# Sorted experts on four places per buffer, and the copy of a tile's gate and up weights split between ScalarE and VectorE

## The reference

```
h = jax.nn.silu(flat @ W1[e]) * (flat @ W3[e])
out = out + cw[:, e:e + 1] * (h @ W2[e])
```

```
act_BSEF = jax.nn.silu(gating_BSEF)
fuse_BSEF = act_BSEF * up_BSEF
out_BSD = jnp.einsum('BSED,BSE->BSD', down_BSED, full_weights_BSE)
```

## Time and profile before

| | us |
|---|---|
| median of 3 runs | 2033.66 (2028.91 to 2034.36) |
| span of the profiled execution | 2032.1 |
| first sorted phase, first load to landing of the last scatter | 1581.2 to 1723.2 |
| second sorted phase, the same | 1860.0 to 2001.3 |

### The profile page before, as it was taken

How to read it: one execution, slowest core, us unless ns; L and a number is a source line. 1 busy time by engine, 2 the same in 40 slices (tenths; PEclk the granted TensorE clock), 3 DMA queues, 4 the chain that set the end, 5 groups by cost and what they waited for, 6 DMA issues and landing times. The chain is left out here.

```text
span 2032.1 us, 46788 instructions
## 1 busy us (share of the span) xinstructions
PE 1596.6 (79%) x16783; PEld 1170.4 (58%) x16783; DVE 1134.2 (56%) x3048; ACT 850.6 (42%) x1634; POOL 564.9 (28%) x782
## 2 busy tenths in 40 slices
PE   5788999999488879699987777888886787343892
PEld 3645666666266647488875454555553686332882
DVE  5755677776554447355544586867773343642333
ACT  2322456555211125244423265655552675002663
POOL 4111011111111103433202211232333354464553
PEclk9989899999699989799988897988895899556996
DMA  4000222221099100000001002222220242211224
GB/s 171 1 2 16 63 59 54 59 58 33 20 323 325 39 1 1 2 4 3 3 2 64 1 1 74 68 68 63 70 56 21 70 113 74 94 49 45 73 75 145
DMA packets 84683, 124.99 MB, mean 62 GB/s; under 512 B 17328, under 2 KB 70576, under 8 KB 82928
## 3 DMA queue, kind: packets, MB, share of 16 engines
q1 hardware_dynamic: 75824, 104.30, 17.6%
q0 software_dynamic: 8640, 17.78, 2.7%
HBM read 67.47 MB, written 55.59 MB: 61 GB/s over the span
## 5 line engine op out<-in xcount | busy, mean ns | idle before, releaser
L1527 DVE TENSOR_REDUCE small<-ps 128x8 f32<-128x1024 f32 (+1 forms) x256 | 312.7, 1224 | 120.6 <-PE ps L1313 70.7
L1454 ACT ACTIVATE scr<-ps 128x1024 f32<-128x1024 f32 x256 | 262.3, 1024 | 237.3 <-PE ps L1288 121.4
L244 POOL TENSOR_TENSOR rstd<-vare,neghalf 128x4 f32<-128x4 f32 (+1 forms) x72 | 63.3, 879 | 542.4 <-DVE vare L223 541.1
L2812 POOL DMA_INDIRECT results<-scr x142 | 136.3, 960 | 154.7 <-DVE scr L2801 67.2
L1326 PE MATMUL ps<-scr 128*32 128x256 f32 x2048 | 173.9, 414 | 0.2 <-ACT scr L1454 0.2
L1275 PEld LDWEIGHTS ps<-scr_r 32*128 32x128 f32 x1024 | 82.3, 195 | 154.9 <-ACT scr L1454 87.6
L1275 PE MATMUL ps<-scr_r 32*128 32x256 f32 x1024 | 136.4, 345 | 35.0 <-ACT scr L1454 21.5
L2733 PE MATMUL ps<-scr 128*128 128x128 f32 x1136 | 155.6, 281 | 2.4 <-ACT scr L2760 1.4
L1306 PE MATMUL ps<-scr_r 32*128 32x256 f32 x1024 | 137.9, 351 | 10.5 <-DMA scr_r<-scr_r 5.9
L2733 PEld LDWEIGHTS ps<-scr 128*128 128x128 f32 x1136 | 142.8, 197 | 3.9 <-issue 3.8
L2794 DVE TENSOR_TENSOR scr<-ps,scr 128x256 f32<-128x256 f32 x142 | 60.3, 425 | 138.2 <-ACT scr L2779 107.6
(11 more groups left out here) (410 smaller groups left out, 3537.0 us busy)
## 6 DMA issues: line engine op xcount, KB each, us to landing
scr_r<-scr_r SPq DMA_DIRECT2D x512, 64.0 KB
rows_m<-kinds SPq DMA_DIRECT2D x8, 2064.0 KB, 30.7
rows_f<-kinds SPq DMA_DIRECT2D x8, 2064.0 KB, 74.9
scr<-results SPq DMA_DIRECT2D x32, 256.0 KB
scr<-rows_m SPq DMA_DIRECT2D x71, 64.5 KB
scr<-rows_f SPq DMA_DIRECT2D x71, 64.5 KB
scr<-in_l3m SPq DMA_DIRECT2D x1, 3072.0 KB, 10.0
results<-scr POOLq DMA_INDIRECT x142
```

What stands on the lines that cost most here:

```text
L244: pool.tensor_tensor(k.rstd[:, 0:self.J], k.vare[:, 0:self.J], k.neghalf[:, 0:self.J], ALU.pow).then_inc(self.e["rstd_ready"].sem, 1)
L1454: act.activation(PT[:, g % 2, 2 * x:2 * x + 2, :], ps[:, 4:6, :], ACT.Exp).then_inc(e["prob_ready"].sem, 1)
L1527: dve.tensor_reduce(nf[:, half, 0:blocks, at:at + 2].rearrange("p q a -> p a q"), ps[:, 2 * (p % 2):2 * (p % 2) + 2, :].rearrange("p a (q ...
L2812: pool.indirect_dma_start(results, bass.IndirectOffsetOnAxis(ap=names[:, j % IN, P:P + 1], axis=0), y[:, j % OUT, :], None).then_inc(store ...
```

## The change

It does these things, all in `phase_sorted_experts`:

- `xT`, `sil`, `hT` and `here` get four places (`DEEP = 4`), `xin` 16 instead of 8. `here` and `y` move to another SBUF region. `turned` and the gate and up products get three PSUM banks each, the projections keep two.
- TensorE's order becomes gate and up of tile j, transposition of j + 4, projection of j - 3.
- ScalarE copies only the gate half of the weights (128 x 256), for tile j + 3, after SiLU j, and copies the transposed rows of j + 3 before SiLU j.
- VectorE copies the up half (128 x 256), with its own register load, for tile j + 3, after the product of tile j and before the eviction of tile j - 3. The up products wait for it by a new semaphore, `up_kept`.

The core of the diff:

```diff
-    e = k.signals(SORTED, turned=1, xt_ready=1, kept=1, gu_ready=1, act_ready=1, h_ready=1, out_ready=1, out_read=1)
-
-    IN, OUT = 8, 4
+    e = k.signals(SORTED, turned=1, xt_ready=1, kept=1, up_kept=1, gu_ready=1, act_ready=1, h_ready=1, out_ready=1, out_read=1)
+
+    IN, OUT, DEEP = 16, 4, 4
...
-    xin, xT, sil, hT, y, here = k.carve((IN, P + 1), (2, P), (2, 2 * P), (2, 2 * P), (OUT, P), (2, 2, 2 * P))
+    xin, xT, sil, hT = k.carve((IN, P + 1), (DEEP, P), (DEEP, 2 * P), (DEEP, 2 * P))
+    here, y = k.carve((DEEP, 2, 2 * P), (OUT, P), base=k.scr2[:, 6144:8704])
...
+    def turned_at(j):
+        return ps[:, j % 3, 0:P]
+    def hidden_at(j):
+        return ps[:, 3 + j % 3, :]
+    def out_at(j):
+        return ps[:, 6 + j % 2, 0:P]
...
         def turn(j):
             arrived(pe, j)
-            wait(pe, "xt_ready", j - 2)
-            pe.transpose(ps[:, j % 2, 0:P], xin[:, j % IN, 0:P], cst["ident"]).then_inc(e["turned"].sem, 1)
+            wait(pe, "xt_ready", j - 3)
+            pe.transpose(turned_at(j), xin[:, j % IN, 0:P], cst["ident"]).then_inc(e["turned"].sem, 1)
 
         def gate_up(j):
             wait(pe, "xt_ready", j)
             wait(pe, "kept", j)
-            wait(pe, "h_ready", j - 2)
+            wait(pe, "h_ready", j - 3)
             for n in range(2):
+                if n:
+                    wait(pe, "up_kept", j)
...
-        for j in range(-2, SORTED + 1):
+        for j in range(-4, SORTED + 3):
             if there(j):
                 gate_up(j)
-            if there(j + 2):
-                turn(j + 2)
-            if there(j - 1):
-                project(j - 1)
+            if there(j + 4):
+                turn(j + 4)
+            if there(j - 3):
+                project(j - 3)
...
-            wait(act, "gu_ready", j - 2)
-            act.activation(here[:, j % 2], gate_up_of[:, :, bass.ds(at, 256)], ACT.Copy).then_inc(e["kept"].sem, 1)
+            wait(act, "gu_ready", j - DEEP)
+            act.activation(here[:, j % DEEP, 0, :], gate_up_of[:, 0, bass.ds(at, 256)], ACT.Copy).then_inc(e["kept"].sem, 1)
...
-        for j in range(-2, SORTED):
+        for j in range(-3, SORTED):
...
+            if there(j + 3):
+                keep_turned(j + 3)
             if there(j):
                 wait(act, "gu_ready", j)
-                wait(act, "h_ready", j - 2)
-                act.activation(sil[:, j % 2, :], ps[:, 2 + j % 2, 0:256], ACT.Silu).then_inc(e["act_ready"].sem, 1)
-            if there(j + 2):
-                keep_turned(j + 2)
-                keep_weights(j + 2)
+                wait(act, "h_ready", j - DEEP)
+                act.activation(sil[:, j % DEEP, :], hidden_at(j)[:, 0:256], ACT.Silu).then_inc(e["act_ready"].sem, 1)
+            if there(j + 3):
+                keep_weights(j + 3)
 
     def dve(dve):
+        dve.wait_ge(arrive, 16 * pieces)
+
+        def keep_up(j):
+            at = dve.value_load(d.table[0:1, 0, j:j + 1], min_val=0, max_val=7 * 256)
+            wait(dve, "gu_ready", j - DEEP)
+            dve.tensor_copy(here[:, j % DEEP, 1, :], gate_up_of[:, 1, bass.ds(at, 256)]).then_inc(e["up_kept"].sem, 1)
+
+        for j in range(DEEP - 1):
+            keep_up(j)
         d.shift(dve)
-        for j in range(SORTED + 1):
+        for j in range(SORTED + 3):
...
+            if there(j + 3):
+                keep_up(j + 3)
```

More of the change, by code:

```diff
@@ L2707, in arrived @@
             eng.wait_ge(loads[j % 4].sem, loads[j % 4].at(j // 4))
+    def turned_at(j):
[4 more added lines that the diff above has]
+        return ps[:, 6 + j % 2, 0:P]
     def sp(sp):
         for j in range(SORTED):
[L2711 to L2712 removed]
+            if load and j >= 16 and j % 4 == 0 and j < 16 + 4 * PIECES:
+                load(sp, (j - 16) // 4)
             row = sp.value_load(d.table[0:1, 1, j:j + 1], min_val=0, max_val=8 * ROWS + 6 * P)
@@ L2729, in gate_up @@
             wait(pe, "kept", j)
-            wait(pe, "h_ready", j - 2)
+            wait(pe, "h_ready", j - 3)
             for n in range(2):
+                if n:
+                    wait(pe, "up_kept", j)
                 for c in range(2):
-                    ins = pe.matmul(ps[:, 2 + j % 2, 256 * n + P * c:256 * n + P * c + P],
-                                    here[:, j % 2, n, P * c:P * c + P], xT[:, j % 2, :], start=True, stop=True)
+                    ins = pe.matmul(hidden_at(j)[:, 256 * n + P * c:256 * n + P * c + P],
+                                    here[:, j % DEEP, n, P * c:P * c + P], xT[:, j % DEEP, :], start=True, stop=True)
             ins.then_inc(e["gu_ready"].sem, 1)
@@ L2792, in dve @@
                 wait(dve, "act_ready", j)
-                wait(dve, "out_ready", j - 2)
-                dve.tensor_tensor(hT[:, j % 2, :], ps[:, 2 + j % 2, 256:512], sil[:, j % 2, :],
+                wait(dve, "out_ready", j - DEEP)
+                dve.tensor_tensor(hT[:, j % DEEP, :], hidden_at(j)[:, 256:512], sil[:, j % DEEP, :],
                                   ALU.mult).then_inc(e["h_ready"].sem, 1)
-            if there(j - 1):
-                wait(dve, "out_ready", j - 1)
-                landed(dve, j - 1 - OUT)
-                out = ps[:, 4 + (j - 1) % 2, 0:P]
+            if there(j + 3):
+                keep_up(j + 3)
+            if there(j - 3):
+                wait(dve, "out_ready", j - 3)
+                landed(dve, j - 3 - OUT)
+                out = out_at(j - 3)
                 if scale is None:
-                    ins = dve.tensor_copy(y[:, (j - 1) % OUT, :], out)
+                    ins = dve.tensor_copy(y[:, (j - 3) % OUT, :], out)
                 else:
-                    ins = dve.tensor_tensor(y[:, (j - 1) % OUT, :], out, scale, ALU.mult)
+                    ins = dve.tensor_tensor(y[:, (j - 3) % OUT, :], out, scale, ALU.mult)
                 ins.then_inc(e["out_read"].sem, 1)
```

10 lines of the change are left out of this document (4 added, 6 removed).

## The result

The changed kernel took **2046.08 us** (median of 6 runs, 2037.64 to 2055.41) beside 2034.01 us for the kernel before (6 runs): a ratio of 1.0078, 95% interval 1.0046 to 1.0109. Slower by 12 us where 27 us less were forecast, and outside the range. The profiled execution has a span of 2044.6 us beside 2032.1.

The account below looks back on a forecast made before the run. SyncE's load queue was taken as the next bound at 1.67 us a tile: 33.0 us of scatter waits, less 4 coming back and 2 for the ends, save 27 us of 2033.7, giving 2006.7 us (range 1992 to 2028).

Parts of the forecast that it names:

- SyncE's queue as the next bound, 1.67 us a load: Sorted phases: SyncE's issue of one load per tile bounds next at 1.67 us, above TensorE's 1.45 us.
- 0.51 us: SyncE's loads: what a POOL call was said to cost SyncE, 1.67 less 1.16 us a load.
- the 33 us of waits: SyncE's waits for scatters in both sorted phases, 15.9 + 17.1 us, all taken to go with 16 places.
- The waits for scatters vanish: SyncE's queue: with 16 places of `xin`, all waits for scatters go, 33.0 us, of which 4 us comes back.
- TensorE goes on through a hold: TensorE works on while its finished products are seen late, about 2.3 us; the added places cover two tiles, 2.9 us.
- The register load at 0 us: VectorE's register load before its new copy runs ahead on the sequencer: counted 0, 0.3 us if it doesn't.
- The copies at 0.40 and 0.29 us: The 128x256 weight copies: 0.40 us on ScalarE (0.38 to 0.63), 0.29 us on VectorE (0.21 to 0.43).
- The ends, 1 us a phase: Longer pipeline behind the last load of each sorted phase: 1 us added a phase, 2 in all (0 to 4).
- Holds stop TensorE as before: Rival: TensorE can't work on while its signals are seen late, 1.80 us a tile stay; 2029 us, chance 0.12.
- TensorE's pace: Rival: evenly spaced POOL calls disturb SyncE less, TensorE bounds at 1.45 to 1.50 us a tile; 1993 us, chance 0.12.
- the copy waiting for POOL: Rival: each VectorE copy waits out a whole POOL call, up to 0.96 us; 2041 us, chance 0.08.
- 0.80 for faster: Chance of a faster time by over 6 us: forecast 0.48, TensorE's pace 0.12, slower SyncE 0.20.

Follow-up runs that it names:

- e13_before: The kernel before, unchanged, profiled on chip 6, which has no late signals: 1.650 and 1.558 us a tile, phases of 125.9 and 122.4 us.
- e1_in16: The kernel before with only `xin` raised from 8 to 16 places, on chip 7 without late signals: ratio 0.9915 to the kernel before.
- e12_whole_first_lag2: Changed kernel with whole weight copies on ScalarE, VectorE's eviction before its product, projection two tiles behind; chip 11, no late signals: ratio 0.9914 to the kernel before.

## Why the prediction was wrong, step by step

- **SyncE's queue as the next bound, 1.67 us a load: wrong, and the step that failed first.** I divided the time of 55 loads, less their visible waits, by 55, and called it SyncE's own cost. From the seventeenth load to the last the same queue with 16 places takes 76.2 us in the first phase on chip 7, 1.41 a load, and 31 of the 54 distances are 1.14 to 1.17 us at one POOL call a tile; on chip 15 the same program takes 96.0 us, 1.78 a load. So 0.51 us was not the price of a POOL call, which next to nothing shows on chip 7: it was the slow steps, two of which stand in the 2.63 us of the earlier trace rows (1649.94 to 1650.67 and 1650.69 to 1651.41). And SyncE, slow as it was, bounded nothing: from the seventeenth on its loads are 13 to 19 us ahead of their transpositions with 16 places on chip 15, and 6 to 11 us in the changed kernel, where the prediction had at most 2, and the time stays. The sum rested on this step: the 33 us of waits were not on the path of a chip with holds. What set the pace there was the holds, 1.8 us a tile with them and 1.45 on the chips without.
- **The waits for scatters vanish: no.** Those of the first 16 loads do (17.3 us for them, 19 forecast). But SyncE soon is 16 tiles ahead of scatters that come no faster, and waits again: 14.1 + 13.1 us in the two phases of the changed kernel, where 15.9 + 17.1 were the earlier trace rows. A wait tells where the queue stands, not what it costs: taking away the places' limit was worth 18 us where signals are on time (phases of e13_before to e1_in16, on two chips) and nothing where they are late.
- **TensorE goes on through a hold: half right.** It did, for two tiles as forecast (2.7 us from the end of the held products to the last start, 2.9 forecast), but the hold was now 2.8 us and not 2.3, and then it stopped as before. I compared the cover with the hold alone and left out the way from its end to the next projection: 1.93 us for SiLU, product, register load, copy and eviction. I counted places and banks and checked what ScalarE has ready; I didn't ask in what order VectorE frees the projection's two banks. The hold got longer and more frequent, which no row of before could tell.
- **The register load at 0 us: wrong.** It is the 0.33 us of idle time before about half of the copies (12.2 us before 58 of them). Where it shows, product to copy is 0.75 us and not 0.34; from product to product VectorE takes 0.89 to 1.40 us when it catches up, where 0.83 was forecast. That is about what ScalarE took before the split (1.26 us). The price I had named for this, 0.3 us, was right, and it fell on the path once a round.
- **The copies at 0.40 and 0.29 us:** 0.418 and 0.351 in the mean. VectorE's takes 0.29 alone, and up to 0.53 beside a POOL call.
- **The ends, 1 us a phase: too low.** They take 3.1 and 2.6 us more on the first chip, 3.0 and 3.2 on chip 6. With the projection two tiles behind and the other two edits (e12_whole_first_lag2) they take 1.0 us more than before.
- **The rivals.** "Holds stop TensorE as before" (2029 us, 0.12) is what happened, with the ends added, and longer holds. "TensorE's pace" (1993 us, 0.12) is what happens on the other kind of chip: 12.5 us less in the phases there, since the kernel before is faster too. The one on the slower side, the copy waiting for POOL, names the right engine and the wrong reason: no POOL call is longer than 1.09 us in the sorted phases of any run, and copies are stretched by 0.25 us at most. By the rule of the Trainium skill ("SBUF — State Buffer", § Who interferes with whom) the second comer is blocked until the first one's instruction ends; the runs agree that there is interference, 0.25 us, but show no wait as long as a call.
- **The chances.** 0.80 for faster came from taking the holds as one candidate and SyncE as the other, and giving them 0.12 and 0.68. The rows for the holds were plain: 20.7 us of SiLU's idle time, in the same row from which the pace was read.

What stays open: what makes the signals late and SyncE slow at the same times, and why only on some chips; why the changed kernel meets more holds; how much of its loss is the copy and how much the order on VectorE, since under holds each was only tried alone, and on a chip where the changed kernel itself didn't run.

## What to carry to other kernels

That a queue is busy all the time doesn't make it the next bound, and its rate on one chip needn't be its cost: look at how far it is ahead of who uses its loads, look at its instructions one by one, and change the depth alone. When places are added to let an engine run on past a late signal, follow the chain from that signal to every bank the engine needs next, in the order in which the freeing engine does its work; work added ahead of the freeing instruction stands on that way. And a change that is meant to cover stalls must be timed on more than one chip, since the stalls may be a chip's.

## What the runs showed of the hardware

- Two kinds of chips, 3% apart on the same program (2034 to 2038 us and 1969 to 1974). About half is in the sorted phases (139.7 + 139.1 us against 125.9 + 122.4). The other half, 31.8 us, lies ahead of them (first load at 1581.2 and 1549.4). The clock accounts for 19 us of it in one stretch there, with the same work in both chips: TensorE is busy for 90% of it on either, but its granted clock is 0.85 on one and 1.00 on the other (windows of the kernel before, first chip, then chip 6):

```profile
1420.00:1545.00 125.00, 112.20 (x1188) 68.67 (x1192) 82.82 (x194) 69.13 (x107) 40.35 (x74) 0.85 0.21 55
...
1405.90:1512.00 106.10, 95.20 (x1184) 59.56 (x1182) 81.37 (x189) 68.81 (x107) 40.11 (x73) 1.00 0.24 65
```

125.0 x 0.85 is 106.3 us, so the clock explains all of the difference in this stretch: parts of the stretch ran at 1.2 GHz on the first chip, none that shows on chip 6. In the 60 tiles of the sorted phases the granted clock is 1.00 on both, and what is late there is the signal.

- Late signals come in order and in a burst: in the round above the products of three tiles, issued 1.45 us apart, have their signals recorded at 1706.65, 1706.83 and 1707.02, and ScalarE takes them at 1.29 and 0.92 us. They recur in whole tiles (13 matmul records each): mostly 7.8 us apart in the first phase of the changed kernel (52 records), mostly 5.0 to 5.1 us in that of the changed kernel on chip 8 (39 records), and 4.8 to 23 us in the kernel before, 12.6 twice (91 and 92 records). The main stream of instruction fetches among the DMA packets has distances of 11 to 16 us in the steady parts and doesn't fall together with them. What else could set the distance was not tried.
- With them SyncE's instructions slow down, to one each 0.7 us: 17 to 64 slow steps from the seventeenth load to the last of a phase on the chips with late signals, none or one on the others.
- A wait of TensorE for its own last signal, ahead of a register load, costs 1.07 us a tile, of which 0.88 us lie between the signal and the projection.
- A register load on VectorE that stands ahead of a copy shows as 0.33 us of idle time before it when the engine comes to it directly from the product (1707.83, 1709.12), and not always (1710.10 has none).
